# Grouped expert layer: every gate tile projected beside the sort, the last two token groups placed between search rounds and at the head of the dense block

## The chip, the cores and the metric

The kernel runs on one core of a Trainium2 chip. The metric is the device time of one execution in microseconds (us). Five engines work side by side: TensorE (PE, with its weight loads as PEld), VectorE (DVE), ScalarE (ACT), GpSimd (POOL) and SyncE (SP); SP and ACT also issue the DMAs spoken of here. "Tile" below means a 128 x 512 float32 block: 128 hidden units for 512 tokens.

## What is computed

Four layers of attention and feed-forward run one after the other over 4096 tokens of width 128. The change touches the feed-forward of the third layer only, a mixture of 64 experts with 32 hidden units each, all experts computed for every token, and the scores of most (group, expert) pairs set to zero:

```python
def _L2_ffn_ref(x, Wr, br, Wup, bup, Wgate, bgate, Wdown, bdown):
    E, H, G, K = (64, 32, 64, 16)
    def _grouped_routing_scores(router_scores):        # (T, En)
        Tq = T // G
        order = jnp.argsort(-router_scores, axis=0)    # each expert sorts its tokens
        sorted_vals = jnp.take_along_axis(router_scores, order, axis=0)
        group_score = sorted_vals.reshape(Tq, G, En).sum(axis=1)
        _, top_flat = jax.lax.top_k(group_score.reshape(-1), Tq * K)
        ...                                            # mask of the chosen groups, back in token order
        fs = jnp.where(mask, router_scores, 0.0)
        return fs / (fs.sum(axis=-1, keepdims=True) + 1e-06)
    router_scores = jax.nn.softmax(xt @ Wr + br, axis=-1)
    fs = _grouped_routing_scores(router_scores)
    up = jnp.einsum('td,edh->teh', xt, Wup) + bup
    gate = jnp.einsum('td,edh->teh', xt, Wgate) + bgate
    h = jax.nn.silu(up) * gate * fs[:, :, None]
    return jnp.einsum('teh,ehd->td', h, Wdown) + fs @ bdown
```

## The kernel before

`grouped_ffn` first normalises the tokens and takes the router's scores. Then two blocks follow, each a program per engine, with a barrier between them.

**The sort block** (names `gr_...`, L1778 to L1957). DVE sorts every expert's scores with a merge network, exchanges halves through four matmuls (`psW`), merges on, and then searches the threshold in ten rounds: a round counts with nine candidate values (`tried`), PE adds the counts over all partitions with one small matmul (`psC`, L1946), and DVE narrows the value (`won`, `cur`). Three questions to PE (`psR`) and a tail of DVE passes over 2048 elements end the block. Beside that, PE projects tiles (`multiply_group`, L1934): the hidden units are 16 steps of 128, in four chunks of four steps, and a chunk holds seven tiles: up and gate of its first three steps and up of the fourth (`kind_of`, `TILES = 7`; tile number 6, `WAITING`, is the up without its gate). ACT takes each tile from PSUM (four banks of `psV`) into the SBUF `ring` with its bias, with silu on the ups (L1814). The tokens are eight groups of 512; a group is 28 tiles. SP spills each finished chunk of a group to DRAM (L1784). The order of groups is 1 to 7, then 0, so that group 0 stays in the ring. On PE groups 1 to 7 stand ahead of the `psW` matmuls and all 28 tiles of group 0 between `psW` and the ten rounds.

**The dense block** (L1990 to L2116). DVE splits the scores into three bf16 parts (`part`), and SP and ACT each send half of them to `parts` (`send_factors`); PE waits for all twelve of these DMAs. Then `pipelined` runs 128 steps, 16 to a group, each engine two or three steps apart: PE spreads the scores over the hidden units with one matmul (`psF`, L2085, `pick` and `parts`), POOL multiplies up by gate from the ring (`tp`, L2012, three steps of each chunk, one chunk ahead), DVE multiplies that by `psF` into `h` (L2048), and PE multiplies `h` into the output (`psY`, L2101, four matmuls). For the fourth step of a chunk PE projects the gate itself (`psG`, L2080) ahead of its `psF`, and DVE adds the bias and multiplies by the waiting up (`tg`, L2037). `h` has two buffers, `psF` four. At a group's start PE also does four `psN` matmuls (L2093) and four for the output bias (L2097), and DVE adds the finished group into the residual. ACT issues the reload of a ring slot (`gr_ring<-gr_spill`, L2002) once POOL and DVE have consumed its chunk (`pooled`, `gated`); apart from that ACT is idle here.

Of the kernel before, what the change touches and what calls it, by code (L numbers as in the profile page):

```python
# [13 lines left out]
ALU = mybir.AluOpType  # L14
# [7 lines left out]
P = 128  # L22
# [1675 lines left out]
def grouped_ffn(nc, m, t):  # L1698
# [8 lines left out]
    with ExitStack() as own:  # L1707
# [12 lines left out]
        CHUNKS, TILES = 4, 7  # L1720
        GROUPS2 = NT // 4
        WAITING = 6
        kind_of = [(0, True), (0, False), (1, True), (1, False), (2, True), (2, False), (3, True)]
# [7 lines left out]
        with ExitStack() as routing:  # L1731
# [46 lines left out]
            with nc.Block() as block:  # L1778
                @block.sync
                def _(sp):  # L1780
                    with sp.Fori(1, GROUPS2) as g:
                        for u in range(CHUNKS):
                            sp.wait_ge(taken, CHUNKS * TILES * (g - 1) + TILES * (u + 1))
                            sp.dma_start(spilled_to(CHUNKS * g + u), slot_of(u)).then_inc(spilled[u], 16)  # L1784
# [13 lines left out]
                def _(act):  # L1798
# [7 lines left out]
                    def take_group(turn):  # L1806
                        for j in range(CHUNKS * TILES):
                            u, (k, is_up) = j // TILES, kind_of[j % TILES]
                            c = 4 * u + k
                            act.wait_ge(multiplied, CHUNKS * TILES * turn + j + 1)  # L1810
# [5 lines left out]
                    take_group(0)  # L1816
                    with act.Fori(1, GROUPS2 - 1) as turn:
                        take_group(turn)
# [4 lines left out]
                    take_group(GROUPS2 - 1)  # L1823
# [92 lines left out]
                def _(pe):  # L1916
# [10 lines left out]
                    def multiply_group(turn, g):  # L1927
                        x = m.xT[:, bass.ds(512 * g, 512)]
                        for j in range(CHUNKS * TILES):
                            u, (k, is_up) = j // TILES, kind_of[j % TILES]  # L1930
                            c = 4 * u + k
                            w = (wu if is_up else wg)[:, EC * c:EC * c + EC, :].rearrange("p e h -> p (e h)")
                            wait_past(pe, taken, CHUNKS * TILES * turn + j - 3)
                            pe.matmul(psV[:, j % 4, :], w, x, start=True, stop=True).then_inc(multiplied, 1)  # L1934

                    multiply_group(0, 1)
                    with pe.Fori(1, GROUPS2 - 1) as turn:
                        multiply_group(turn, turn + 1)
# [4 lines left out]
                    multiply_group(GROUPS2 - 1, 0)  # L1943
                    for k in range(ROUNDS):
                        pe.wait_ge(counted, k + 1)
                        pe.matmul(psC[:, 0:TRIED], mats[:, ALL, :], tried[:, :], start=True, stop=True).then_inc(total_ready, 1)  # L1946
                    pe.wait_ge(asked, 1)
# [594 lines left out]
```

## Time and profile before

| what | us |
|---|---|
| median of three runs | 2104.02 (2103.9 to 2107.18) |
| the profiled execution: its own time | 2103.53 |
| its span, first to last instruction | 2101.6 |
| sort block's tiles and sort, to the last tile | 1146.8 to 1342.7 |
| search rounds | 1343.0 to 1363.4 |
| rest of the sort block | 1363.8 to 1387.0 |
| dense block: until the score parts land | 1387.4 to 1402.2 |
| dense block: 128 steps | 1402.2 to 1622 |

Times within the program are counted from the span's start. A matmul of float32 operands is recorded as two passes, so 28 tiles are 56 matmul records. Busy time of a pipelined engine overlaps itself; distances between starts are the safer numbers.

### The profile page before, as it was taken

The page shows a single profiled execution, that of the slowest core. Times are in us where ns is not written, and L with a number is a line of the kernel's source. Part 1 is how long each engine was busy: PE and PEld are TensorE (multiplying, and loading weights), DVE is VectorE, ACT ScalarE, POOL GpSimd, SP SyncE. Part 2 cuts the span into 40 slices and gives each one's busy share as a digit, 9 for nine tenths or more (in the row PEclk, how much of TensorE's full clock was granted, in tenths as well). Part 3 has the DMA queues.
Part 4 walks back from the last instruction along what each step waited for, and adds up shares of the span by engine and source line. Part 5 has one row for each costly group of instructions (what it writes and reads, how often), then busy time and mean ns, then how long its engine had stood idle before and what let it go on. Part 6 is the DMA issues. An engine that isn't in the chain of part 4 may idle for free. (4 is left out here: it accounts for less than half of the span.)

```text
span 2101.6 us, 46036 instructions
## 1 busy us (share of the span) xinstructions
PE 1615.8 (77%) x14574; PEld 1131.0 (54%) x14579; DVE 1420.2 (68%) x3509; ACT 786.4 (37%) x1658; POOL 820.8 (39%) x809
## 2 busy tenths in 40 slices
PE   5999935634888879986885999639998887179992
PEld 4777732223666646654763444327776666055551
DVE  6888867766787644466886999666556687953332
ACT  4555524687333323323433887400000443122221
POOL 3888804294332250063320000015554331037883
PEclk9999987855899799996997999859999799555555
DMA  5333304900111511111114777137774121334446
GB/s 140 80 79 79 78 24 131 274 1 21 40 47 30 179 41 43 40 41 49 54 40 83 304 314 301 48 85 280 275 257 144 45 57 55 97 69 82 81 82 148
DMA packets 242439, 226.80 MB, mean 108 GB/s; under 512 B 105698, under 2 KB 225314, under 8 KB 234914
## 3 DMA queue, kind: packets, MB, share of 16 engines
q1 hardware_dynamic: 217042, 154.96, 24.6%
q10 hardware_dynamic: 10960, 55.87, 7.6%
q0 software_dynamic: 14336, 14.69, 3.9%
q8 instruction: 55, 0.90, 0.2%
q14 instruction: 46, 0.38, 0.1%
HBM read 129.94 MB, written 92.90 MB: 106 GB/s over the span
## 5 line engine op out<-in xcount | busy, mean ns | idle before, releaser
L643 POOL TENSOR_TENSOR at_KM<-at_K,at_mask 128x512 f32<-128x512 f32 x96 | 99.8, 1040 | 307.0 <-PE at_psS L668 244.1
L718 ACT ACTIVATE at_ET<-at_psT 128x512 f32<-128x512 f32 x192 | 114.6, 597 | 248.9 <-PE at_psT L677 248.9
L2012 POOL TENSOR_TENSOR gr_work<-gr_ring 128x512 f32<-128x512 f32 x96 | 121.5, 1277 | 104.3 <-DVE gr_work L2048 97.1
L753 DVE TENSOR_REDUCE at_mx<-at_psS 128x16 f32<-128x1024 f32 x96 | 117.6, 1225 | 57.1 <-PE at_psS L668 56.8
L2101 PEld LDWEIGHTS gr_psY<-gr_wd,gr_work 128*128 128x128 f32 x1024 | 134.8, 196 | 38.7 <-DVE gr_work L2048 22.3
L2101 PE MATMUL gr_psY<-gr_wd,gr_work 128*128 128x128 f32 x1024 | 142.4, 283 | 10.2 <-DVE gr_work L2048 10.1
L400 POOL TENSOR_TENSOR at_E<-at_Z,at_mx 128x512 f32<-128x512 f32 x128 | 130.8, 1043 | 44.1 <-PE at_psT L445 28.4
L690 PE MATMUL at_psO<-at_VZ,at_ET 128*64 128x18 f32 x3072 | 111.9, 216 | 39.9 <-ACT at_ET L718 39.8
L677 PE MATMUL at_psT<-kept_ident,at_Z 128*128 128x128 f32 x768 | 132.4, 298 | 10.4 <-DVE at_Z L766 5.2
L690 PEld LDWEIGHTS at_psO<-at_VZ,at_ET 128*64 128x64 f32 x3072 | 103.1, 143 | 58.4 <-ACT at_ET L718 37.0
L1934 PE MATMUL gr_psV<-kept_xT,gr_wu 128*128 (+1 forms) x256 | 125.9, 592 | 0.8 <-ACT gr_V L1803 0.8
L258 ACT ACT_TABLE_LOAD x6 | 7.7, 1283 | 304.9 <-PEq L63 299.6
L677 PEld LDWEIGHTS at_psT<-kept_ident,at_Z 128*128 128x128 f32 x768 | 85.0, 147 | 55.3 <-issue 40.9
L518 DVE TENSOR_TENSOR at_Z<-at_psS,at_amask 128x512 f32<-128x512 f32 x128 | 82.4, 686 | 41.3 <-PE at_psS L437 40.3
L2336 POOL DMA_INDIRECT cap_acc<-cap_Y,cap_idx x64 | 101.9, 1592 | 20.7 <-issue 19.5
L2048 DVE TENSOR_TENSOR gr_work<-gr_psF,gr_work 128x512 f32<-128x512 f32 x128 | 85.6, 685 | 34.8 <-PE gr_psY L2101 19.6
L2013 POOL MEMSET gr_one<- 64x1 f32 x1 | 0.1, 91 | 255.5 <-POOLq L1778 255.5
L2330 POOL DMA_INDIRECT cap_GX<-cap_rows,cap_idx x64 | 63.3, 989 | 90.6 <-DVE cap_idx L2369 77.8
L2375 DVE TENSOR_TENSOR cap_h<-cap_psU,cap_sg 64x128 f32<-64x128 f32 x64 | 18.1, 283 | 118.5 <-ACT cap_sg L2389 118.5
L1934 PE MATMUL gr_psV<-kept_xT,gr_wg 128*128 (+1 forms) x192 | 98.0, 592 | 0.0
L1814 ACT ACTIVATE gr_ring<-gr_psV,gr_bu 128x512 f32<-128x512 f32 x128 | 88.0, 688 | 21.5 <-PE gr_psV L1934 21.5
L768 DVE TENSOR_TENSOR at_Z<-at_psS,at_mx 128x512 f32<-128x512 f32 x128 | 82.4, 686 | 6.6
(550 smaller groups left out, 4195.1 us busy)
## 6 DMA issues: line engine op xcount, KB each, us to landing
gr_spill<-gr_ring SPq DMA_DIRECT2D x28, 1792.0 KB, 5.7
gr_ring<-gr_spill ACTq DMA_DIRECT2D x28, 1792.0 KB, 7.1
at_amask<-mask_Bx16xSxS_ff SPq DMA_DIRECT2D x128, 128.0 KB, 2.9
kv_values<-bit_VS SPq DMA_DIRECT2D x32, 432.0 KB, 6.6
at_VZ<-kv_values SPq DMA_DIRECT2D x96, 144.0 KB, 2.2
kv_keys<-bit_KS SPq DMA_DIRECT2D x8, 768.0 KB, 6.9
at_K<-kv_keys SPq DMA_DIRECT2D x96, 64.0 KB, 1.9
cap_acc<-cap_zero SPq DMA_DIRECT2D x2, 2112.0 KB, 12.6
```

What stands on the lines that cost most here:

```text
L400: pool.tensor_tensor(E[:, a, :].rearrange("p (v k) -> p v k", k=SEQ), Z[:, s % 2, a, :].rearrange("p (v k) -> p v k", k=SEQ), mx[:, s % 2, ...
L643: pool.tensor_tensor(KM[:, s % 2, :, :], K[:, s, :].unsqueeze(1).broadcast_to([P, 4, P]), mask4[:, :].unsqueeze(2).broadcast_to([P, 4, P]) ...
L677: last = pe.transpose(psT[:, r * P:r * P + P], Z[:, a, r * P:r * P + P], m.ident[:, :])
L690: last = pe.matmul(psO[rows, t * PW:t * PW + PW], ET[:, 4 * a + r, rows], VZ[:, s, PAIRS * b + t, :, :].rearrange("p j w -> p (j w)"), sta ...
L718: act.activation(ET[:, 4 * a:4 * a + 4, :].rearrange("p r q -> p (r q)"), psT[:, :], ACT.Exp, scale=QK_SCALE).then_inc(exped, 1)
L753: dve.tensor_reduce(mx[:, :].rearrange("p (g v) -> p g v", v=4), psS[:, :, 0:256].rearrange("p g (v k) -> p g v k", k=SEQ), AX.X, ALU.max) ...
L1814: act.activation(ring[:, u, j % TILES, :], psV[:, j % 4, :], ACT.Silu if is_up else ACT.Identity, bias=bias).then_inc(taken, 1)
L1934: pe.matmul(psV[:, j % 4, :], w, x, start=True, stop=True).then_inc(multiplied, 1)
L2012: pool.tensor_tensor(tp[:, s % 4, :], ring[:, s // 4, first, :], ring[:, s // 4, first + 1, :], ALU.mult).then_inc(pooled, 1)
L2048: dve.tensor_tensor(h[:, s % 2, :], psF[:, s % 4, :], product_of, ALU.mult).then_inc(h_ready, 1)
L2101: last = pe.matmul(psY[:, j, :], h[:, s % 2, j * P:j * P + P], wd[:, s, :], start=False, stop=(s == C - 1), skip_group_check=True)
L2336: pool.indirect_dma_start(accs[s % ACCS], bass.IndirectOffsetOnAxis(ap=idx2[:, s:s + 1], axis=0), Y[:, s % 4, :], None, compute_op=ALU.add ...
```

## The change

`TILES` is 8 instead of 7: the gate of the fourth step (`OTHER = 7`) is projected in the sort block with the rest, so a group has 32 tiles and a spilled chunk is 128 x 4096 instead of 128 x 3584. Groups 1 to 6 (192 tiles) stand ahead of the `psW` matmuls. Group 7 and the first 16 tiles of group 0 are handed out by `last_two`: 18 ahead of the rounds, 2 after each of the first six rounds' `psC`, 1 after each of the last four, then 2, 4 and 8 after the three questions. The last 16 tiles of group 0 stand at the head of the dense block's PE program, through `psF`, and ACT takes them between its sends of the score parts. SP instead of ACT issues the reloads. In the steps, `psG` is filled by an ACT copy from the ring (`copy_gate`), and DVE's `tg` is a plain product. `rest` and `tg` move from `work` to `ctxT`, which holds nothing that is still needed.

```diff
-        CHUNKS, TILES = 4, 7
+        CHUNKS, TILES = 4, 8
         GROUPS2 = NT // 4
-        WAITING = 6
+        WAITING, OTHER = 6, 7
+        ALL_TILES, LATE_TILES = CHUNKS * TILES, 16
+        AHEAD, PER_ROUND, AFTER = 18, (2, 2, 2, 2, 2, 2, 1, 1, 1, 1), (2, 4, 8)
...
+                    def last_two(first, count):
+                        for n in range(first, first + count):
+                            if n < ALL_TILES:
+                                multiply(GROUPS2 - 2, GROUPS2 - 1, n)
+                            else:
+                                multiply(GROUPS2 - 1, 0, n - ALL_TILES)
+
+                    last_two(0, AHEAD)
                     for k in range(ROUNDS):
                         pe.wait_ge(counted, k + 1)
                         pe.matmul(psC[:, 0:TRIED], mats[:, ALL, :], tried[:, :], start=True, stop=True).then_inc(total_ready, 1)
+                        last_two(AHEAD + sum(PER_ROUND[:k]), PER_ROUND[k])
...
                 @block.scalar
                 def _(act):
-                    send_factors(act, 1)
-                    with act.Fori(1, GROUPS2) as g:
-                        for u in range(CHUNKS):
-                            act.wait_ge(pooled, 3 * C // 4 * (g - 1) + 3 * u + 3)
-                            act.wait_ge(gated, C // 4 * (g - 1) + u + 1)
-                            act.dma_start(slot_of(u), spilled_to(CHUNKS * g + u)).then_inc(back[u], 16)
+                    def take_late(count):
+                        for n in range(count - 5 if count > 5 else 0, count):
...
+                            act.wait_ge(late_multiplied, n + 1)
...
+                    send_scores(act, 1)
+                    take_late(1)
+                    for n in range(3):
+                        send_part(act, 1, n)
+                        take_late(5 * n + 6)
+
+                    def copy_gate(q, s, g):
+                        if s % 4 == 3:
+                            wait_past(act, back[s // 4], 16 * g)
+                            wait_past(act, gated, ones_of(s, g) - 2)
+                            act.activation(psG[:, s // 4 % 2, :], ring[:, s // 4, OTHER, :], ACT.Copy).then_inc(gate_up, 1)
+
+                    run(act, [(2, copy_gate)])
...
                         if s % 4 == 3:
-                            dve.wait_ge(up_ready, q + 1)
-                            wait_past(dve, back[s // 4], 16 * g)
+                            dve.wait_ge(gate_up, ones_of(s, g))
                             wait_past(dve, h_ready, q - 3)
-                            dve.scalar_tensor_tensor(tg[:, s // 4 % 2, :], psG[:, s // 4 % 2, :], bg[:, s:s + 1], ring[:, s // 4, WAITING, :],
-                                                     ALU.add, ALU.mult).then_inc(gated, 1)
+                            dve.tensor_tensor(tg[:, s // 4 % 2, :], psG[:, s // 4 % 2, :], ring[:, s // 4, WAITING, :], ALU.mult).then_inc(gated, 1)
...
                     def up(q, s, g):
                         wait_past(pe, h_ready, q - 3)
-                        x = m.xT[:, bass.ds(512 * g, 512)]
-                        if s % 4 == 3:
-                            pe.matmul(psG[:, s // 4 % 2, :], wg[:, EC * s:EC * s + EC, :].rearrange("p e h -> p (e h)"), x, start=True, stop=True)
...
+                    for n, j in enumerate(late_tiles):
...
+                        wait_past(pe, late_taken, n - 3)
+                        pe.matmul(psF[:, j % 4, :], w, m.xT[:, 0:512], start=True, stop=True).then_inc(late_multiplied, 1)
+                    pe.wait_ge(late_taken, LATE_TILES)
```

PE before, from the last tile ahead of the search through the rounds to the second question:

```order
L1934 MATMUL gr_psV<-kept_xT,gr_wu 128x512
L1946 MATMUL gr_psC<-gr_tried,gr_mats 128x9 x10
L1948 MATMUL gr_psR<-gr_cols,gr_mats 128x1
L1949 MATMUL gr_psR<-gr_cols,gr_mats 128x1
L1950 MATMUL gr_psR<-gr_eq,gr_mats 128x32
L1951 MATMUL gr_psR<-gr_eq,gr_mats 128x32
L1953 MATMUL gr_psR<-gr_cols,gr_mats 128x1
```

PE in the change, from the last two-tile round to the first question:

```order
L1958 MATMUL gr_psC<-gr_tried,gr_mats 128x9
L1936 MATMUL gr_psV<-kept_xT,gr_wu 128x512
L1936 MATMUL gr_psV<-kept_xT,gr_wg 128x512
L1958 MATMUL gr_psC<-gr_tried,gr_mats 128x9
L1936 MATMUL gr_psV<-kept_xT,gr_wu 128x512
L1958 MATMUL gr_psC<-gr_tried,gr_mats 128x9
L1936 MATMUL gr_psV<-kept_xT,gr_wg 128x512
```

Ten `psC` in a row have become ten `psC` with one or two tiles behind each.

PE before, at the head of the dense block and in its first steps:

```order
L2085 MATMUL gr_psF<-gr_parts,gr_pick 128x512 x3
L2093 MATMUL gr_psN<-gr_one,gr_fst 128x1 x4
L2097 MATMUL gr_psY<-gr_bd,gr_fst 128x128 x4
L2101 MATMUL gr_psY<-gr_wd,gr_work 128x128 x4
L2080 MATMUL gr_psG<-kept_xT,gr_wg 128x512
L2085 MATMUL gr_psF<-gr_parts,gr_pick 128x512
L2101 MATMUL gr_psY<-gr_wd,gr_work 128x128 x4
```

PE in the change, at the same place:

```order
L2151 MATMUL gr_psF<-kept_xT,gr_wu 128x512
L2151 MATMUL gr_psF<-kept_xT,gr_wg 128x512
L2126 MATMUL gr_psF<-gr_parts,gr_pick 128x512 x3
L2134 MATMUL gr_psN<-gr_one,gr_fst 128x1 x4
L2138 MATMUL gr_psY<-gr_bd,gr_fst 128x128 x4
L2142 MATMUL gr_psY<-gr_wd,gr_work 128x128 x4
L2126 MATMUL gr_psF<-gr_parts,gr_pick 128x512
L2142 MATMUL gr_psY<-gr_wd,gr_work 128x128 x4
```

The `psG` matmul is gone from the steps, and late tiles (the last two of sixteen are shown) stand ahead of the first `psF`.

ACT in the change, at the head of the dense block:

```order
L2003 DMA gr_fs<-gr_V 64x2048
L2032 ACTIVATE gr_ring<-gr_psF,gr_bu 128x512
L2009 DMA gr_parts<-gr_part 32x2048 x2
L2032 ACTIVATE gr_ring<-gr_psF,gr_bg 128x512
L2032 ACTIVATE gr_ring<-gr_psF,gr_bu 128x512
L2032 ACTIVATE gr_ring<-gr_psF,gr_bg 128x512
L2032 ACTIVATE gr_ring<-gr_psF,gr_bu 128x512
L2032 ACTIVATE gr_ring<-gr_psF,gr_bg 128x512
L2009 DMA gr_parts<-gr_part 32x2048 x2
```

Before, one `gr_fs` DMA and six `gr_parts` DMAs followed each other there; now takes of late tiles stand between the pairs.

## Rows read from the trace of the kernel before

**Rows 1.** Waits, dense block's steps: who waited for whom, us in total, times, longest

```profile
DVE gr_work L2037 <- PE gr_psF L2085: 60.4, 32, 7.4
PEld gr_psY L2101 <- DVE gr_work L2048: 22.3, 32, 0.9
```

**Rows 2.** Stages: length, busy us per engine (records), granted clock, DMA share, GB/s

```profile
1318.70:1342.70 24.00, 24.00 (x57) 10.64 (x56) 16.29 (x17) 19.69 (x29) 0.00 (x0) 1.00 0.10 41
1343.00:1363.40 20.40, 4.97 (x19) 4.09 (x18) 15.59 (x53) 0.63 (x1) 0.00 (x0) 0.61 0.00 0
1363.80:1387.00 23.20, 3.94 (x16) 3.63 (x16) 19.38 (x30) 0.00 (x0) 0.00 (x0) 0.50 0.00 0
1387.40:1402.20 14.80, 0.00 (x0) 0.00 (x1) 8.52 (x5) 0.00 (x0) 3.96 (x4) 0.50 0.86 177
1403.60:1433.10 29.50, 28.51 (x170) 23.19 (x169) 13.90 (x24) 0.00 (x0) 15.54 (x13) 0.85 0.58 205
1433.10:1511.60 78.50, 73.79 (x505) 59.54 (x504) 47.01 (x93) 0.00 (x0) 45.61 (x37) 1.00 0.77 282
```

**Rows 3.** Timeline of one chunk in the dense steps: start, us, engine, line, operation [idle <-releaser]

```profile
1501.47 1.08 PEld L2101 LDWEIGHTS gr_psY<-gr_wd,gr_work 128*128 128x128 f32 x8 [0.33 <-issue]
...
1501.89 0.75 DVE L2037 SCALAR_TENSOR_TENSOR gr_work<-gr_psG,gr_bg,gr_ring 128x512 f32<-128x512 f32 x1 [1.43 <-PE gr_psF L2085]
...
1503.29 0.97 PEld L2101 LDWEIGHTS gr_psY<-gr_wd,gr_work 128*128 128x128 f32 x8 [0.72 <-DVE gr_work L2048]
...
1504.29 1.08 PEld L2101 LDWEIGHTS gr_psY<-gr_wd,gr_work 128*128 128x128 f32 x8
1504.51 1.05 PE L2101 MATMUL gr_psY<-gr_wd,gr_work 128*128 128x128 f32 x8
...
1505.40 1.08 PEld L2101 LDWEIGHTS gr_psY<-gr_wd,gr_work 128*128 128x128 f32 x8
...
1505.67 0.69 DVE L2048 TENSOR_TENSOR gr_work<-gr_psF,gr_work 128x512 f32<-128x512 f32 x1 [0.42 <-PE gr_psY L2101]
...
1507.37 1.08 PEld L2101 LDWEIGHTS gr_psY<-gr_wd,gr_work 128*128 128x128 f32 x8 [0.33 <-issue]
```

**Rows 4.** Timeline of PE: the first matmuls of four of the eight groups

```profile
1403.60 1.86 PE L2093 MATMUL gr_psN<-gr_one,gr_fst 64*128 64x1 f32 x8
...
1433.07 1.05 PE L2093 MATMUL gr_psN<-gr_one,gr_fst 64*128 64x1 f32 x8
...
1485.35 1.05 PE L2093 MATMUL gr_psN<-gr_one,gr_fst 64*128 64x1 f32 x8
...
1511.61 1.05 PE L2093 MATMUL gr_psN<-gr_one,gr_fst 64*128 64x1 f32 x8
```

**Rows 5.** Timeline of the search: first count, first two answers, last answer

```profile
1335.44 0.46 DVE L1871 TENSOR_REDUCE gr_tried<-gr_reach 128x9 f32<-128x288 f32 x1
...
1343.06 0.17 DVE L1876 SCALAR_TENSOR_TENSOR gr_won<-gr_psC,gr_cand 128x9 f32<-128x9 f32 x1 [6.84 <-PE gr_psC L1946]
...
1344.73 0.39 PE L1946 MATMUL gr_psC<-gr_tried,gr_mats 128*128 128x9 f32 x2 [1.71 <-DVE gr_tried L1871]
1345.16 0.17 DVE L1876 SCALAR_TENSOR_TENSOR gr_won<-gr_psC,gr_cand 128x9 f32<-128x9 f32 x1 [0.16 <-PE gr_psC L1946]
...
1363.37 0.17 DVE L1876 SCALAR_TENSOR_TENSOR gr_won<-gr_psC,gr_cand 128x9 f32<-128x9 f32 x1 [0.69 <-PE gr_psC L1946]
```

**Rows 6.** The page's costliest groups: ACT's takes of up tiles, mean ns

```profile
L1814 ACT ACTIVATE gr_ring<-gr_psV,gr_bu 128x512 f32<-128x512 f32 x128 | 88.0, 688 | 21.5 <-PE gr_psV L1934 21.5
```

**Rows 7.** Head, dense block: PE's first matmul (timeline); ACT's sends (line), ns min/median/max

```profile
1402.23 1.44 PE L2085 MATMUL gr_psF<-gr_parts,gr_pick 96*128 96x512 bf16 x3 [26.04 <-DMA gr_parts<-gr_part]
...
L1988 ACTq DMA_DIRECT2D gr_parts<-gr_part x6: 586/702/2363, 1388.7 to 1395.3; - x6
```

**Rows 8.** DMA issues: reloads, KB, median us to landing; stage view of one us

```profile
gr_ring<-gr_spill ACTq DMA_DIRECT2D x28, 1792.0 KB, 7.1
...
1507.00:1508.00 1.00, 1.00 (x7) 0.64 (x6) 0.21 (x1) 0.00 (x0) 0.82 (x1) 1.00 1.07 459
```

## What the change was predicted to do

> **What bounds the kernel now.** I read the stages first, then the waits of the dense block, then one chunk of its timeline, then the search. Nothing outside this layer is touched, so only 1146 to 1622 us counts.
>
> In the dense steps PE is the bound: it is busy 73.8 of 78.5 us at full clock [rows 2], and the two long waits there hang on it. DVE's gate product waits 60.4 us in 32 times for the `psF` that stands behind `psG` on PE, and PE in turn waits 22.3 us for DVE, again 32 times, once per chunk [rows 1]. One chunk shows how [rows 3]. PE's output loads of undisturbed steps start 1.11 apart (1504.29, 1505.40). The step with `psG` takes 1.97 (1505.40 to 1507.37), so `psG` costs 0.86. Then `psF` comes, then DVE's gate (0.75) and product, and PE's next load starts 1.82 after the one before it, having idled 0.72; the step behind it takes 1.00, so the wait costs 0.60 net. 4 x 1.11 + 0.86 + 0.60 = 5.90, the distance from 1501.47 to 1507.37. A group is 26.26 long [rows 4], four chunks of 5.90 and 2.66 for its start.
>
> In the search it is PE's order that binds: the first count is ready at 1335.90, but its answer comes at 1343.06, after 6.84 of idle DVE [rows 5], because 28 tiles stand ahead of it; 24.00 us for 28 tiles is 0.857 a tile [rows 2]. After that, ten rounds run with PE idle 1.71 of each 2.10 [rows 5], and at the head of the dense block PE does nothing for 14.8 us until the score parts land [rows 2, 7].
>
> **The change part by part.** All is summed against the profiled execution (2103.53 us, 0.5 below the median of the three runs).
>
> Ahead of the exchange there are 192 tiles instead of 196. PE gets there 4 x 0.857 = 3.4 us sooner, and DVE's sort, which PE then waits for, is unchanged: nothing gained.
>
> Ahead of the search: 18 tiles instead of 28 end ten tiles, 8.6 us, before 1342.70, at 1334.1, and so before the first count. The answer follows a count on an idle PE by 0.43 (1344.73 to 1345.16 [rows 5]): 1336.3 instead of 1343.06, **-6.7**.
>
> The rounds: the nine from first to last answer take 20.31, a mean of 2.26, while the first takes 2.10 [rows 5]; the later ones run at a granted clock that falls from 2.4 to 1.2 GHz as PE idles (mean 0.61 of the stage, 0.50 behind it [rows 2]). Two tiles are 1.71, just the idle time of a round, so at full clock they fit with nothing to spare, and a busier PE should hold the clock: 9 x 2.10 = 18.9, **-1.4**. With the clock at 1.2 GHz two tiles take 3.43 and a round 1.7 us more.
>
> The questions: ahead of each there is a DVE stretch long enough for its 2 or 4 tiles; behind the third, 8 tiles (6.9) lie beside the rest of DVE's 19.4 us. PE's 3.94 us of small matmuls there ran at 0.50 [rows 2]; at best half of it returns, mostly hidden: **-0.5**, ends 0 and -2. If that cover failed (8 tiles at half clock, 13.7), the block would end 2 or 3 us later.
>
> PE now idles twice where it did not: about 3 us ahead of the exchange (DVE's sort ends when it did) and 2 ahead of the first count. If the clock falls in such a gap, the four exchange matmuls (as long as four tiles, 3.4 us) or a round take up to twice as long. Ends 0 and +7; I take **+2**.
>
> The head of the dense block: DVE's splitting, and so SP's half of the sends, are as before. ACT's half is queued behind takes of late tiles, at 0.69 each [rows 6], and PE waits for both. ACT now does: the first take (PE's first tile 1.0 and 0.7 with the send of the scores beside it, say 1.8), a pair of sends, five takes (3.4), a pair, five takes (3.4), a pair. A send takes 0.70 by the median and 2.36 at most [rows 7]. With medians the last send is issued at 1.8 + 1.4 + 3.4 + 1.4 + 3.4 + 0.7 = 12.1; with the two long sends of before at 14.8. Before it was issued at 1395.3, 7.9 after the block's start, and PE began 6.9 later [rows 7]. So the parts land 4.2 to 6.9 later; PE's own 16 tiles (13.7) and the last five takes end inside that at full clock. At half clock throughout, the tiles take 27.4: +13. I take **+6**, near the end with long sends, since their queue carries the same bytes.
>
> The first group: it took 29.47 against 26.26 [rows 4], at a mean clock of 0.85 [rows 2], since PE came out of 26 us of idling. Now it comes out of 16 tiles and a short wait: **-3.2**, or 0 if the clock falls in that wait.
>
> The dense steps: `psG` is gone (0.86 a chunk), and the gate no longer waits for PE but for an ACT copy, about 0.6 to 0.7 us like ACT's other tiles [rows 6], that runs up to two chunks ahead; ACT is otherwise idle there. What is late next is DVE itself. A step's product ends 2.07 after the output load of two steps before it began (load 1504.29, its matmuls' end 1505.56, product 1505.67 to 1506.36 [rows 3]), and PE needs it 2.22 after, so DVE has 0.15 to spare. A gate of 0.69 set between two products, each 0.69 after the other, ends the second at 2.07 + 0.70 + 0.69 + 0.05 = 3.5 against 3.33 needed: 0.18 late, of which PE wins back up to 0.11 in the next step, as it does now. I take 0.15 a chunk. POOL's three products (some 3.9 us) fit a chunk. A group becomes 4 x (4.44 + 0.15) + 2.66 = 21.0.
>
> The reloads, now on SP, have eight tiles, 2.10 MB instead of 1.84. No row shows several queued. At the best rate of a reload, 459 GB/s [rows 8], one takes 4.6 us; at the stage's mean scaled to a full share (282 / 0.77 = 366 [rows 2]), 5.7. The chunk with its part of the group's start is 5.25. I take a value nearer the fast end, since the slow one counts each lone reload's slow beginning, and add 0.2 a group: 21.2. Over eight groups 8 x (26.26 - 21.2) = **-40.5**.
>
> The Trainium skill (DMA: Bandwidth & Descriptors, "Where 436 GB/s comes from") says that between HBM and SBUF the HBM side binds at about 358 GB/s for a core. By that a reload would take 5.9 us and a group 23.4. The row of 459 GB/s speaks against it as a ceiling for a lone core; it is the second rival's mechanism.
>
> The spill in the sort block grows by the same eighth, but a chunk there takes 8 tiles instead of 7, so its rate stays.
>
> Sum: -6.7 - 1.4 - 0.5 + 2 + 6 - 3.2 - 40.5 = -44.3; 2103.5 - 44.3 = 2059.2, and 2059.7 beside the median.
>
> **The rivals.** First, the gate's wait comes back in another form: the change would remove PE's matmul but not the stall, because gate and product still stand back to back on DVE. For it: DVE's spare time is 0.15 a step, all of it worked out from modelled ends of matmuls. Against it: the gate can now start as soon as DVE is free. With 0.60 a chunk instead of 0.15, 32 x 0.45 = 14.4: 2074.
>
> Second, the reloads become the bound: at 5.7 us each a group is 22.9 in the seven groups that are reloaded, 7 x 1.7 = 12: 2072. For it: the DMA share is 0.77 already [rows 2], for an eighth less data in a quarter more time. Against it: no engine waits for a reload now, and POOL runs a chunk ahead with four slots.
>
> Third, the clock: if it is at 1.2 GHz through the six two-tile rounds (+10), the head (+7) and the first group (+3), the time is 2080. For it: the rounds' and the head's clock now [rows 2]. Against it: PE has over 80% of those rounds to work.
>
> Fourth, on the other side: reloads that follow each other with their whole latency. One lands after 7.1 us [rows 8]; with 8/7 of the bytes, at most 8.1, a group 32.5, 7 x 11.3 = 79: 2139. It turns the change into a loss from 6.9 us a reload on (7 x (27.5 - 21.2) eats the 44). Against it: now one is issued every 5.90 and lands after 7.1, so two already overlap.
>
> Last, more than forecast: no gate stall, no reload term, no clock lost in gaps, the head at its short end (4.8 + 1.6 + 2 + 1.8): 2049.5.
>
> **How the numbers follow.** The forecast (2052 to 2066 on its own) 0.55; gate stall 0.12; reload pace 0.15; clock 0.10; serial reloads 0.03; more than forecast 0.05. The range reaches from below the last case to the clock's: 2047 to 2080. About 0.2% (4.2 us) is what a measurement of this kernel can tell from no change. Slower takes the serial reloads and a remainder of what I don't see, 0.04; within 0.2%, 0.02; faster 0.94.
>
> **What would show it.** After: no `psG` matmul from PE in the steps; starts of groups about 21 us apart (22.7 and a PE wait for DVE once a chunk would be the first rival, POOL or ACT waiting for a DMA the second); first answer of the search about 0.4 after the first count, and rounds of 2.1 with the clock at 1.00; the parts landing about 21 us after the dense block's start, with ACT's sends the last; the first group no longer than the others. The prediction is wrong where the tiles placed in the search make the rounds longer than 2.3, or where the head costs more than the search gives.

## Result and profile after

The changed kernel takes 2053.28 us (median of four runs) where the kernel before took 2105.60 beside it: a ratio of 0.974 [0.971, 0.978], 52 us less. Run again later it gave 0.972 [0.969, 0.975], 62 us less by the medians. The forecast was 2059.7.

Whole times of one kernel spread over some 20 us here, since the granted clock of stages whose code was not touched differs from run to run (from 280 to 310 us it was 0.70 to 1.00 in the profile of before and 0.50 to 0.53 in that of after). Over all profiles this layer starts between 1140.8 and 1154.2 us. So the layer's own length, from ACT's first copy into `gr_V` to the first transposition of the norm behind it, decides below. It went from 482.6 to 420.5: **62.1 less, where the sum said 44.3**. In the profiled execution the same code took 9.1 longer ahead of the layer and 4.8 longer behind it, so its span fell by 48.2 only.

Stages of the changed kernel (length, busy us of PE, PEld, DVE, ACT, POOL with records, granted clock, DMA share, GB/s), to be held against [rows 2]: 18 tiles, rounds, questions, head, first group, the next six groups.

```profile
1328.00:1343.00 15.00, 15.00 (x36) 6.65 (x37) 13.68 (x13) 12.31 (x19) 0.00 (x0) 1.00 0.33 140
1346.10:1365.40 19.30, 17.05 (x51) 7.39 (x52) 15.82 (x53) 10.30 (x15) 0.00 (x0) 1.00 0.51 218
1365.80:1388.00 22.20, 18.20 (x46) 8.07 (x44) 19.41 (x30) 10.31 (x15) 0.00 (x0) 0.85 0.11 48
1388.50:1404.80 16.30, 15.50 (x32) 6.51 (x32) 7.46 (x5) 10.28 (x17) 4.09 (x4) 0.91 0.76 161
1405.60:1425.50 19.90, 19.90 (x161) 18.84 (x160) 14.14 (x25) 2.58 (x5) 15.48 (x13) 1.00 0.83 306
1425.50:1547.10 121.60, 120.67 (x962) 113.87 (x961) 94.16 (x187) 14.44 (x24) 91.14 (x73) 1.00 1.00 415
```

PE now works through the rounds, the questions and the head, where its clock had been 0.61, 0.50 and 0.50. In the dense steps it is busy 99% at full clock, and the DMA engines are full as well. The waits there (who waited for whom: us in total, times, longest) against [rows 1]:

```profile
ACT gr_psG L2044 <- DVE kept_ctxT L2082: 55.2, 12, 5.6
ACT gr_psG L2044 <- DMA gr_ring<-gr_spill: 52.1, 12, 5.3
POOL gr_work L2058 <- DVE gr_work L2092: 31.0, 37, 1.3
DVE gr_work L2092 <- PE gr_psY L2142: 23.5, 61, 0.5
```

PE's 22.3 us of waiting for DVE is gone; those who wait are ACT, POOL and DVE, none of them the bound. One chunk (start, us, engine, line, operation), against [rows 3]:

```profile
1472.63 1.08 PEld L2142 LDWEIGHTS gr_psY<-gr_wd,gr_work 128*128 128x128 f32 x8
...
1472.90 0.69 DVE L2092 TENSOR_TENSOR gr_work<-gr_psF,gr_work 128x512 f32<-128x512 f32 x1
1473.51 0.68 DVE L2082 TENSOR_TENSOR kept_ctxT<-gr_psG,gr_ring 128x512 f32<-128x512 f32 x1
...
1473.74 1.08 PEld L2142 LDWEIGHTS gr_psY<-gr_wd,gr_work 128*128 128x128 f32 x8
...
1474.11 0.68 DVE L2092 TENSOR_TENSOR gr_work<-gr_psF,gr_work 128x512 f32<-128x512 f32 x1
...
1474.85 1.08 PEld L2142 LDWEIGHTS gr_psY<-gr_wd,gr_work 128*128 128x128 f32 x8
```

PE's loads start 1.11 apart through the gate, with no stall: a chunk is 4 x 1.11 = 4.44. DVE's three operations start 0.61 and 0.60 apart, though each is recorded as 0.68 or 0.69. The head on PE and on ACT, against [rows 7]:

```profile
1388.54 2.05 PE L2151 MATMUL gr_psF<-kept_xT,gr_wu 128*128 128x512 f32 x2 [2.98 <-PEq L1781]
1390.38 1.54 PE L2151 MATMUL gr_psF<-kept_xT,gr_wg 128*128 128x512 f32 x2
...
1403.02 1.02 PE L2151 MATMUL gr_psF<-kept_xT,gr_wg 128*128 128x512 f32 x2
1404.82 0.82 PE L2126 MATMUL gr_psF<-gr_parts,gr_pick 96*128 96x512 bf16 x3 [0.78 <-ACT gr_ring L2032]
```

```profile
1394.74 0.69 ACT L2032 ACTIVATE gr_ring<-gr_psF,gr_bg 128x512 f32<-128x512 f32 x1
1395.31 0.69 ACT L2032 ACTIVATE gr_ring<-gr_psF,gr_bu 128x512 f32<-128x512 f32 x1
1395.50 0.51 ACTq L2009 DMA_DIRECT2D gr_parts<-gr_part  x1
1395.88 0.70 ACT L2032 ACTIVATE gr_ring<-gr_psF,gr_bg 128x512 f32<-128x512 f32 x1
...
1399.79 1.35 ACTq L2009 DMA_DIRECT2D gr_parts<-gr_part  x2
...
1404.08 0.69 ACT L2032 ACTIVATE gr_ring<-gr_psF,gr_bg 128x512 f32<-128x512 f32 x1 [0.17 <-PE gr_psF L2151]
```

What ends the head is ACT's take of the last late tile (PE waits 0.78 for it), no longer the score parts.

### The profile page after: what moved, and what is told of

Its sections match the earlier page's. It is cut to its first block and busy times, and to the rows that moved or that the text cites. A ratio compares the mean times of both kernels' runs of the same rounds, so it can differ in the third digit from the quotient of the medians.

```text
span 2053.4 us, 45919 instructions
## 1 busy us (share of the span) xinstructions
PE 1617.8 (79%) x14578; PEld 1144.2 (56%) x14579; DVE 1418.5 (69%) x3509; ACT 825.6 (40%) x1722; POOL 820.6 (40%) x809
## 5 line engine op out<-in xcount | busy, mean ns | idle before, releaser
L2142 PE MATMUL gr_psY<-gr_wd,gr_work 128*128 128x128 f32 x1024 | 135.8, 276 | 0.0
L1936 PE MATMUL gr_psV<-kept_xT,gr_wg 128*128 (+1 forms) x240 | 124.6, 601 | 0.0
L2384 POOL DMA_INDIRECT cap_acc<-cap_Y,cap_idx x64 | 101.9, 1592 | 20.7 <-issue 18.9
L2423 DVE TENSOR_TENSOR cap_h<-cap_psU,cap_sg 64x128 f32<-64x128 f32 x64 | 18.1, 282 | 119.7 <-ACT cap_sg L2437 119.7
L1817 ACT ACTIVATE gr_ring<-gr_psV,gr_bu 128x512 f32<-128x512 f32 x120 | 82.4, 687 | 31.3 <-PE gr_psV L1936 31.3
L1817 ACT ACTIVATE gr_ring<-gr_psV,gr_bg 128x512 f32<-128x512 f32 x120 | 82.4, 687 | 23.6 <-PE gr_psV L1936 23.2
L2092 DVE TENSOR_TENSOR gr_work<-gr_psF,gr_work 128x512 f32<-128x512 f32 x96 | 66.0, 688 | 33.1 <-PE gr_psY L2142 22.9
## 6 DMA issues: line engine op xcount, KB each, us to landing
gr_ring<-gr_spill SPq DMA_DIRECT2D x28, 2048.0 KB, 10.2
```

The costliest lines, as they stand in the source:

```text
L1817: act.activation(ring[:, u, j % TILES, :], psV[:, j % 4, :], ACT.Silu if is_up else ACT.Identity, bias=bias).then_inc(taken, 1)
L1936: pe.matmul(psV[:, j % 4, :], w, m.xT[:, bass.ds(512 * g, 512)], start=True, stop=True).then_inc(multiplied, 1)
L2142: last = pe.matmul(psY[:, j, :], h[:, s % 2, j * P:j * P + P], wd[:, s, :], start=False, stop=(s == C - 1), skip_group_check=True)
L2384: pool.indirect_dma_start(accs[s % ACCS], bass.IndirectOffsetOnAxis(ap=idx2[:, s:s + 1], axis=0), Y[:, s % 4, :], None, compute_op=ALU.add ...
```

## Experiments

Each row is one profile, in us. First answer and block start count from the layer's start; the head runs from there to the first `gr_psN` matmul; the seven groups from there to the last of the eight `gr_psN` records with which the eighth group begins, 0.8 after that group's start. The ratio is to the kernel before, run on the same chip, with its 95% interval.

| kernel | first answer | block starts | head | seven groups | layer | ratio |
|---|---|---|---|---|---|---|
| before | 199.6 | 243.9 | 16.2 | 191.5 | 482.6 | |
| after | 193.9 | 235.9 | 17.1 | 142.3 | 420.5 | 0.974 [0.971, 0.978] |
| e0_changed_again | 192.5 | 234.1 | 18.1 | 142.3 | 419.7 | 0.972 [0.969, 0.975] |
| e1_unplaced | 229.7 | 274.0 | 16.1 | 148.0 | 463.4 | 0.988 [0.981, 0.995] |
| e6_placement_alone | 192.9 | 237.6 | 16.1 | 189.2 | 473.8 | 0.996 [0.994, 0.998] |
| e2_matmul_back | 192.4 | 234.1 | 18.1 | 166.4 | 447.3 | 0.986 [0.978, 0.993] |
| e9_wait_back | 192.4 | 234.1 | 18.1 | 162.3 | 441.8 | 0.982 [0.974, 0.990] |
| e8_gate_from_sbuf | 192.4 | 234.1 | 18.1 | 147.7 | 425.2 | 0.973 [0.970, 0.976] |
| e4_reload_nine | 192.4 | 234.1 | 18.0 | 148.3 | 428.0 | 0.974 [0.971, 0.978] |
| e3_reload_seven | 192.4 | 234.1 | 18.0 | 142.3 | 419.6 | 0.964 [0.960, 0.968] |
| e5_no_late | 204.3 | 246.5 | 16.1 | 145.3 | 433.0 | 0.974 [0.970, 0.978] |
| e7_gaps_filled | 195.1 | 237.1 | 15.2 | 147.2 | 424.7 | 0.975 [0.971, 0.978] |
| e10_late_thirteen | 192.3 | 234.6 | 15.5 | 145.5 | 420.8 | 0.970 [0.966, 0.974] |
| e11_kept_busy | 192.5 | 234.7 | 15.5 | 142.3 | 417.8 | 0.967 [0.962, 0.973] |

The lengths of the first seven groups, from the starts of their first `gr_psN` matmuls, as in [rows 4]:

```
before              29.47 26.02 26.26 26.26 27.42 27.52 27.72
after               19.95 20.21 20.27 20.27 20.28 20.27 20.27
e2_matmul_back      23.39 23.64 23.72 23.71 23.72 23.71 23.71
e9_wait_back        22.08 22.35 23.05 23.05 23.05 23.98 23.98
e8_gate_from_sbuf   20.59 20.79 20.78 20.77 22.41 20.76 20.77
e4_reload_nine      19.95 20.20 20.41 20.28 22.09 22.53 22.06
e3_reload_seven     19.95 20.21 20.27 20.28 20.27 20.27 20.27
e5_no_late          22.86 20.20 20.28 20.28 20.26 20.28 20.27
e7_gaps_filled      23.18 20.20 20.27 20.28 21.91 20.26 20.27
e10_late_thirteen   23.15 20.20 20.27 20.28 20.27 20.27 20.27
e11_kept_busy       19.95 20.21 20.27 20.28 20.27 20.27 20.27
```

**The two halves of the change.** In e1 all 64 tiles of the last two groups stand ahead of the search, and the dense steps are as in the change.

```diff
-        ALL_TILES, LATE_TILES = CHUNKS * TILES, 16
-        AHEAD, PER_ROUND, AFTER = 18, (2, 2, 2, 2, 2, 2, 1, 1, 1, 1), (2, 4, 8)
+        ALL_TILES, LATE_TILES = CHUNKS * TILES, 0
+        AHEAD, PER_ROUND, AFTER = 64, (0,) * 10, (0, 0, 0)
...
```

> The changed kernel with all 64 tiles of the last two groups between the exchange and the search, none between the rounds, none behind the questions and none in the dense block. My theory: PE's queue stands ahead of the first count, 64 x 0.857 = 54.9 us behind the exchange, so the first answer comes some 37.6 later than in the changed kernel, the rounds take 2.26 instead of 2.10 as the clock falls, the head is 1 shorter and the first group 3 longer: the layer takes 420.5 + 42 = 462, the kernel 2095. Rival, the tiles cost PE the same wherever they stand and the placement gives at most what DVE's own idle gave, 10: 430.

In e6 the kernel before keeps its gate in the dense steps and spreads its last 28 tiles: 18 ahead of the search, one in each round.

```diff
...
-                    multiply_group(GROUPS2 - 1, 0)
+                    multiply_group(GROUPS2 - 1, 0, range(18))
                     for k in range(ROUNDS):
                         pe.wait_ge(counted, k + 1)
                         pe.matmul(psC[:, 0:TRIED], mats[:, ALL, :], tried[:, :], start=True, stop=True).then_inc(total_ready, 1)
+                        multiply_group(GROUPS2 - 1, 0, range(18 + k, 19 + k))
```

> The kernel before with its seven tiles a chunk and its gate matmuls in the dense block; of the 28 tiles of group 0, 18 stay ahead of the search and one stands behind each round's count. My theory: the first answer comes 6.7 earlier, the rounds take 2.10 instead of 2.26 because PE's clock holds (1.4), the rest stays: the layer takes 474.5 instead of 482.6. Rival, PE's tiles delay the rounds' counts by as much as the first answer gains: 482 or more.

Placement as in e6 (without late tiles and tiles behind the questions) makes the layer 8.8 shorter. The first answer is 6.7 of it, the term as forecast, but the block starts only 6.3 sooner: the rounds took 20.0, not the 18.9 that I expected. With one tile a round the clock did not hold at first, as it did with two in the change (1.00): the first five rounds of e6 ran at 0.55 (stages as above):

```profile
1344.19:1355.60 11.41, 10.66 (x21) 4.33 (x21) 8.99 (x30) 3.04 (x5) 0.00 (x0) 0.55 0.00 1
```

Another 2.3 of the 8.8 is no work of placement: in the dense steps the clock fell in three groups of before (the fifth to the seventh) and in one of e6 (27.82 long). Moving the gates alone gives 19.2: the seven groups win 43.5, but 36 more tiles ahead of the search bring the first answer 30.1 later. Together they give 62.1, more than the sum, because a moved tile is free only in a stretch where PE idled. With such falls of the clock taken out on both sides (3.9 in before, 1.6 in e6, and 1.6 in e1, whose sixth group took 21.91), it is about 58 against 6 and 17. e1's layer (463.4) fits the 462 expected; its whole time, 2083, lay under the expected 2095.

The unchanged changed kernel, run a second time, is the yardstick for all the others:

> The changed kernel once more, to have its layer and its whole time beside the next one's on the same chip. Layer 420.5 within 2 us (its profile before), whole time 2045 to 2064 as its runs so far.

Its layer came out as expected (419.7); its whole times, 2038 to 2054, lay partly below the expected 2045 to 2064.

**What a dense chunk won.** e2 puts a gate matmul back on PE in each chunk, read by nobody; the gate does not wait for it.

```diff
+                        if s % 4 == 3:
+                            pe.matmul(psF[:, s % 4, :], wg[:, EC * s:EC * s + EC, :].rearrange("p e h -> p (e h)"), m.xT[:, bass.ds(512 * g, 512)], start=True, stop=True)
```

> The changed kernel with one more matmul per chunk on PE: the gate's projection, into the psF bank that the next matmul overwrites, so its result is used by nobody. Numbers are for the layer, from ACT's first copy of the scores to the first transposition of the next layer's norm: 482.6 us before, 420.5 changed. My theory, PE alone bounds the dense steps and the wait it lost was a cost of its own: the layer grows by 32 x 0.86 = 27.5 to 448. Rival, the matmul and DVE's wait cannot be had apart (a longer PE step makes the gate late again): 32 x 1.46 = 47, to 467. Rival, the reloads bound the steps and PE has room: less than 10, to under 430.

e9 lets the gate wait for the `psF` behind it again, with no matmul.

```diff
+                            dve.wait_ge(up_ready, q + 1)
                             dve.wait_ge(gate_up, ones_of(s, g))
```

> The changed kernel with the old wait of DVE's gate product on the psF of its own step, and without the gate's matmul on PE. My theory: the gate starts only when PE has issued that psF, 1.11 ahead of the load that needs the product behind it; gate and product take 0.60 + 0.69 + 0.05 from about 0.25 after, so PE is late by some 0.4 a chunk, 13 us, and the layer takes 433. Rival, the wait costs its whole 0.60 as in the kernel before: 440. Rival, the wait was only a symptom of the matmul ahead of psF, and costs nothing without it: 420 to 422.

A group of e2 is 23.71, 3.44 over the changed kernel's 20.27, or 0.86 a chunk: the matmul, as read from [rows 3]. A group of e9 is 23.05 in the middle, 0.69 a chunk. There my expectation (433) fell and its rival (440) held: e9's layer is 441.8. The chunk of e9 shows why:

```profile
1481.88 0.69 DVE L2083 TENSOR_TENSOR kept_ctxT<-gr_psG,gr_ring 128x512 f32<-128x512 f32 x1 [0.72 <-PE gr_psF L2127]
...
1482.49 0.68 DVE L2093 TENSOR_TENSOR gr_work<-gr_psF,gr_work 128x512 f32<-128x512 f32 x1
...
1483.22 0.97 PEld L2143 LDWEIGHTS gr_psY<-gr_wd,gr_work 128*128 128x128 f32 x8 [0.81 <-DVE gr_work L2093]
```

DVE idles 0.72 for PE, then PE 0.81 for DVE. The whole stall came from that wait, none of it from gate and product standing back to back. Matmul and wait add up: seven groups 24.1 and 20.0 longer, 44.1 together, where the change won 49.2. The last two groups of e9, at a clock of 0.93, took 0.93 each over the 23.05, which leaves 42.2; 3.2 of the rest is the first group's clock (below), and 3.9 the falls of the clock in before.

e8 leaves out ACT's copy, and DVE's gate reads both operands from SBUF.

```diff
...
-                            dve.tensor_tensor(tg[:, s // 4 % 2, :], psG[:, s // 4 % 2, :], ring[:, s // 4, WAITING, :], ALU.mult)
+                            dve.tensor_tensor(tg[:, s // 4 % 2, :], ring[:, s // 4, OTHER, :], ring[:, s // 4, WAITING, :], ALU.mult)
```

> The changed kernel without ACT's copy of the gate into PSUM: DVE multiplies the two ring tiles out of SBUF. Theory that the copy is only there for the operand's place: a product of two SBUF tiles takes 0.70 on DVE in the sort, against 0.68 to 0.69 from PSUM, and the layer stays at 420 to 422. Rival, with POOL's products running from the same ring beside it the SBUF product takes longer or holds POOL up: half a us a chunk, 16, 437.

It came out between the two: the gate takes 0.87 by the median and up to 1.38 (columns: ns min/median/max, first and last start) instead of 0.68, and PE waits for DVE again, a quarter of a us at a time:

```profile
L2083 DVE TENSOR_TENSOR kept_ctxT<-gr_ring x32: 680/872/1380, 1402.6 to 1565.2; 128x512 f32<-128x512 f32 x32
```

```profile
PEld gr_psY L2143 <- DVE gr_work L2093: 7.4, 29, 0.4
```

A group is 20.77, so the copy is worth 0.5 a group; another 1.6 of e8's 5.4 is its fifth group, where the clock fell (below).

**The reloads.** e4 brings an extra eighth of each chunk into `gr_V`, unread; e3 leaves an eighth out.

```diff
...
+                            sp.dma_start(extra[:, u, :], spilled_to(CHUNKS * g + u)[:, 0:512]).then_inc(extra_in[u], 16)
                             sp.dma_start(slot_of(u), spilled_to(CHUNKS * g + u)).then_inc(back[u], 16)
```

> The changed kernel with an eighth more to load in the dense block: ahead of each reload SP loads one tile of the same chunk a second time into a buffer that nobody reads. The reloads now move 415 GB/s at a DMA share of 1.00 while PE is busy 99% of the steps. Theory that the DMA has no room: a chunk of 2.36 MB at 415 GB/s is 5.7 us, a group 22.7 instead of 20.3, the layer +17, 437. Theory that it has room to some 440 GB/s: a group 21.4, +8, 429. Theory that PE alone bounds it and the queue absorbs more: 420 to 423.

```diff
-                            sp.dma_start(slot_of(u), spilled_to(CHUNKS * g + u)).then_inc(back[u], 16)
+                            sp.dma_start(slot_of(u)[:, 0:3584], spilled_to(CHUNKS * g + u)[:, 0:3584]).then_inc(back[u], 16)
```

> Each reload of the dense block brings back seven of a chunk's eight tiles; the eighth, the linear half of the gate, stays what it was, so that part of the result is left out. It tells what sets the dense steps of the changed kernel, whose DMA share is 1.00 at 415 GB/s while PE is busy 99 percent. My theory: PE sets them, and the reloads fit with next to nothing to spare. Then the seven groups from first to last start take 142.3 us as before, the layer 420 +-2, and only the reloads' time to landing falls, from 10.2 to 8 or less. Rival: the reloads already set the pace (2.10 MB each 5.07 us is 414 GB/s), then an eighth less lets a group fall below 20.27, the seven groups to 140 or less.

With an eighth less, every group is the same to 0.01: PE sets the pace of the changed kernel, at 414 GB/s (2.10 MB each 5.07 us). The reloads then land after 9.1 by the median, not in 8 or less as I expected. With an eighth more, four groups go by almost unchanged on what the slots hold, and the last three take 22.2 by the mean (POOL's waits for reloads grow from 7.4 us in the first of the two stretches below to 22.1 in the second): 9.44 MB in 22.2 us is 425 GB/s, the rate of the whole stretch of e4 (stages as above):

```profile
1419.00:1479.70 60.70, 60.27 (x480) 56.69 (x480) 46.36 (x93) 6.62 (x11) 42.56 (x35) 1.00 1.01 424
1479.80:1546.40 66.60, 63.45 (x481) 57.31 (x480) 46.14 (x93) 7.22 (x12) 44.47 (x37) 0.97 1.01 423
```

So e4's layer (428.0) fits the expectation with room to spare (429), but the mechanism is a ceiling of about 425 that is felt only late, and some 2 us of the 8.3 over e0 are by my estimate the clock's: it fell to 0.92 in the sixth group (22.5 against 22.1) and in the eighth, where PE was busy 1.65 longer than in the changed kernel. The changed kernel stands 2 to 3% below it. The Trainium skill (DMA: Bandwidth & Descriptors, "Where 436 GB/s comes from") gives about 358 for a core between HBM and SBUF; 424 held over 60 us speaks against it for a lone core. By 358 a group would be 23.4, an estimate from that page's figure.

**The head.** e5 has no late tiles (34 ahead of the search), e7 four tiles ahead of the exchange, 20 ahead of the search and ten late, e10 eleven behind the third question and 13 late, and e11 is e10 with three tiles more at the end of the row, unread.

```diff
-        ALL_TILES, LATE_TILES = CHUNKS * TILES, 16
-        AHEAD, PER_ROUND, AFTER = 18, (2, 2, 2, 2, 2, 2, 1, 1, 1, 1), (2, 4, 8)
+        ALL_TILES, LATE_TILES = CHUNKS * TILES, 0
+        AHEAD, PER_ROUND, AFTER = 34, (2, 2, 2, 2, 2, 2, 1, 1, 1, 1), (2, 4, 8)
...
```

> The sixteen late tiles go ahead of the search (34 there instead of 18), none stands at the head of the dense block; all else as in the changed kernel. My theory: 18 tiles leave PE about 2 us idle ahead of the first count, so 16 more bring the first answer 16 x 0.857 - 2.0 = 11.7 later (192.4 to 204.1 us into the layer); the head falls only from 17.1 or 18.0 to the 16.1 that the score parts need in any case; and PE, idle through it, starts the first group at a granted clock of 0.50, which costs 3 to 6 us in the groups (142.3 to 145 to 148). Layer 419.7 + 11.7 - 1.9 + 3 to 6 = 432 to 436. Rival: the late tiles are what the head waits for, so that without them it shrinks by most of their 13.7 us: head 8 or less, layer 425 or less.

```diff
...
+                    last_two(0, 4)
                     pe.wait_ge(swapped, 1)
...
-                    last_two(0, AHEAD)
+                    last_two(4, AHEAD - 4)
...
```

> The changed kernel with six tiles fewer at the head of the dense block (10 of 16): four more stand ahead of the exchange, two more between it and the search. My theory: PE then idles neither ahead of the exchange (3 us now) nor ahead of the first count (1.6), the exchange takes 3.8 instead of 5.3 since the clock holds, and the head is 2 shorter, since ACT has fewer takes ahead of its last send: layer 420.5 - 1.5 - 2 = 417. Rival, the head is bound by DVE's splitting and the sends and does not shorten, while PE, waiting there, loses its clock for the first group (3): 420 to 423.

```diff
-        ALL_TILES, LATE_TILES = CHUNKS * TILES, 16
-        AHEAD, PER_ROUND, AFTER = 18, (2, 2, 2, 2, 2, 2, 1, 1, 1, 1), (2, 4, 8)
+        ALL_TILES, LATE_TILES = CHUNKS * TILES, 13
+        AHEAD, PER_ROUND, AFTER = 18, (2, 2, 2, 2, 2, 2, 1, 1, 1, 1), (2, 4, 11)
...
```

> Three of the late tiles move behind the third question (11 there instead of 8), where PE idles 2.7 to 4.7 us before the dense block; 13 are left at its head, and ACT takes four instead of five between the pairs of sends. My theory: PE's idle stretch holds them, so the block's start stays at 234.1 to 235.9 us into the layer; the last send goes out three takes (1.8 us) sooner and the last take ends 2.6 sooner; head 15.5 instead of 17.1 to 18.0, and the seven groups keep 142.3, since PE waits 1 us at most for the parts. Layer 417 to 418. Rival: PE now waits for the parts as it did with ten late tiles (2.56 us), and the clock falls to 0.50 at the first group, which gives the gain back: seven groups 145 to 147, layer 420 to 423. In the whole time either is below what three rounds can tell; the layer's own length decides.

```diff
+                    for n in range(LATE_TILES, LATE_TILES + 3):
+                        wait_past(pe, late_taken, n - 3)
+                        pe.matmul(psF[:, n - LATE_TILES, :], wu[:, 0:EC, :].rearrange("p e h -> p (e h)"), m.xT[:, 0:512], start=True, stop=True)
                     pe.wait_ge(late_taken, LATE_TILES)
```

> The thirteen-late-tiles kernel with three more tiles at the end of PE's row at the head, whose results nobody reads: they fill the 2.30 us in which PE waited there for the score parts. It tells whether the first group's 23.15 us (against 19.95 in the changed kernel) came from that idle stretch. My theory: it did; with PE at work until the parts land the granted clock stays at 1.00, the first group takes 19.95, the seven groups 142.3, the head 15.4 to 16.0 and the layer 417.5 to 418.5, the shortest of all kernels here. Rival: the clock falls for another reason (the head's earlier idling, or the small matmuls at the group's start): first group 23 again, layer 421 or more.

The parts need 14 to 15 us whatever PE does: the last one lands 14.3 to 14.7 after the block's start in before, after, e5, e7, e10 and e11. Without late tiles the head is 16.1, with 13 it is 15.5. The sixteen late tiles cost 1 to 2 there; ahead of the search they cost 11.8, and e5's layer (433.0) came out as expected. e7 and e10 made the head shorter, as expected, and lost the gain in the first group, where e10's rival held. PE of e10 waits 2.30 for the parts. Its first three matmuls behind the wait still run at full speed (0.81 for the three, as in e11), then the granted clock is 0.50, which is 1.2 GHz: the eight small matmuls take 1.86 instead of 1.05.

```profile
1396.88 0.81 PE L2126 MATMUL gr_psF<-gr_parts,gr_pick 96*128 96x512 bf16 x3 [2.30 <-DMA gr_parts<-gr_part]
1397.62 1.86 PE L2134 MATMUL gr_psN<-gr_one,gr_fst 64*128 64x1 f32 x8
```

```profile
1397.62:1399.50 1.88, 1.88 (x10) 1.88 (x10) 1.56 (x3) 0.28 (x1) 1.43 (x2) 0.50 0.00 0
```

In e11 three filler tiles take up that wait, and nothing else differs:

```profile
1400.93 2.74 PE L2154 MATMUL gr_psF<-kept_xT,gr_wu 128*128 128x512 f32 x6
1403.67 0.81 PE L2126 MATMUL gr_psF<-gr_parts,gr_pick 96*128 96x512 bf16 x3
1404.41 1.05 PE L2134 MATMUL gr_psN<-gr_one,gr_fst 64*128 64x1 f32 x8
```

First group 23.15 to 19.95: the idle stretch is the cause. e11 has the shortest layer of all, 2.0 under e0; its whole time does not tell it apart from the changed kernel's. e7's layer (424.7) missed both its expectation (417) and its rival (420 to 423). Its other losses were 2.6 up to the first answer, since its four tiles overfilled the gap ahead of the exchange (0.84 in e0), and the 1.6 of its fifth group.

## Why the prediction was right, and where it was not

The time lay 6 us from the forecast, inside its own range, and the reasons held: the gate off PE, its stall gone, the search freed, rounds at full clock. That the number came so near was luck: the layer won 17.8 more than the sum, and stages that nobody touched gave 13.9 of it back in that profile. By the layer, what happened is the prediction's last case, "more than forecast", to which it gave 0.05: no gate stall, no reload term, almost no loss in the gaps, a head below its short end. That case would have made the layer 54.5 shorter (44.3 and 10.2); it was 62.1. By terms of the sum:

- **First answer and the gaps (-6.7, and +2 with ends 0 and +7).** The first answer came 5.7 sooner, 7.1 in most other runs. The difference is one of the two gaps: in the profile of after PE idled 2.75 ahead of the exchange, and its eight matmuls took 5.29; in e0 it idled 0.84 and they took 3.89. The gap ahead of the first count (1.64) cost nothing. Right, +1 instead of +2.

```profile
1323.70 5.29 PE L1946 MATMUL gr_psW<-gr_A,gr_mats 128*128 128x512 f32 x8 [2.75 <-DVE gr_A L1688]
...
1346.08 0.39 PE L1958 MATMUL gr_psC<-gr_tried,gr_mats 128*128 128x9 f32 x2 [1.64 <-DVE gr_tried L1875]
```

- **Rounds (-1.4).** 20.3 to 18.9, at a clock of 1.00: exact. **Questions (-0.5).** -0.9.
- **Head (+6, from +4.2).** It cost 0.9, and 1.8 in e0: below the lower end. The step that failed is "the parts land 4.2 to 6.9 later". ACT's last pair went out from 1399.8 to 1401.1, some 12 after the block's start, as the sum with medians had it, but everything had landed 2.5 after the last send (1400.3 to 1402.8), where before it took 6.4 (1395.7 to 1402.1). Counted from the block's start, the last part came after 14.4, against 14.7 before (15.2 in e0) and the "about 21" that the prediction gave as a sign. Times to landing of all twelve sends in after, over both queues, and of the last pair alone in e0:

```profile
DMA to landing us min/median/max: 2.4/5.3/7.2
```

```profile
DMA to landing us min/median/max: 2.3/2.3/2.3
```

  All twelve sends count up one semaphore. From its first twelfth (8.3 after the block's start before, 7.8 in after) to its last, a twelfth came every 0.58 by the mean before and every 0.59 in after: the sends share one pace, and most of the 6.4 was waiting for the sends ahead. When the last send of before went out, not one twelfth was in; when the last pair of after went out, six were. I had carried the latency of the former over to the latter. This is read from the counts, not tried by itself. Takes also cost less: 0.57 to 0.60 each in a row, not 0.69. The Trainium skill (ScalarE: Activation LUTs, "What ACT_TABLE_LOAD costs") says that ACTIVATEs in a row overlap by about 0.09, which these rows bear out.
- **First group (-3.2).** 29.47 to 19.95. Against the groups that follow, the 3.2 is gone altogether, and e10 and e11 show its cause.
- **Dense steps (-40.5 for eight groups).** A group is 20.27, not 21.2. The gate's remaining stall of 0.15 a chunk is zero: I set gate and product 0.69 apart, while DVE starts them 0.60 apart, which a row of before would have told, two products in 1.28:

```profile
1502.56 1.28 DVE L2048 TENSOR_TENSOR gr_work<-gr_psF,gr_work 128x512 f32<-128x512 f32 x2
```

  The reload's 0.2 is zero (e3), and a group's start costs 2.51, not 2.66. That is 0.93 x 8 = 7.4. Another 3.9 is no work of the change's terms: groups five to seven of before took 27.4 to 27.7 at a granted clock of 0.94, and I had counted each at 26.26.

Of the rivals, the gate's stall did not come back, and e9 shows what would have brought it. The reload's pace is real but lies just behind PE's (e3, e4). The clock's fall is real too, and the late tiles, sixteen and not thirteen, ten or none, are what keep it from the first group. Serial reloads did not occur: a landing of 10.2 with several queued moves 415 GB/s.

```profile
gr_ring<-gr_spill SPq DMA_DIRECT2D x28, 2048.0 KB, 10.2
```

## What to carry to other kernels

Work moved off a bound stage is worth its full price only where it lands in idle time of the same engine; price the two halves together, since e1 and e6 gave 28 of the 62 when made apart (23 of 58 without the falls of the clock). Ahead of a stage that PE bounds, a short wait of PE can cost more than itself: behind waits of 2.30 and 2.56 (e10, e7) the first group ran in part at half the clock, behind waits of 0.78 (after, e0) it did not. Filling the 2.30 with matmuls nobody reads gave 3.2 us back. Take an operation's price in a row from start to start, not from its recorded length.

## What the runs showed of the hardware

The clock also falls without an idle PE. Once in e1, once in e7 and once in e8, in the middle of the dense steps, a group took 1.6 longer at a mean clock of 0.92; this is the stretch of e7, with PE busy 5.94 of 6.10:

```profile
1483.90:1490.00 6.10, 5.94 (x34) 5.47 (x34) 3.78 (x11) 0.60 (x1) 3.18 (x3) 0.72 0.98 403
```

A clock of 0.92 to 0.94 over a group is also seen where PE waits in between: in groups five to seven of before (27.4 to 27.7 against 26.26), in the fifth of e6, the sixth and eighth of e4 and the sixth and seventh of e9. It is seen in none of after, e0, e2, e3, e5, e10 and e11. What sets it off stays open.

Reading from HBM, a lone core kept 423 to 425 GB/s for over 100 us, and 415 beside a PE that was never late. A DVE product with one operand in PSUM took 0.68, the same with both in SBUF 0.87 by the median while POOL, whose three products a chunk read SBUF too, worked beside it. In the sort of before, where POOL has no records, operations of that shape on SBUF operands took 0.69 to 0.70 by the mean. That points to POOL, but it was not tried.
